# Product with the kernel spectrum formed in place of the mixed stream, in two operations of 1024 elements, with spectra two images ahead in two buffers

## The chip, the core and the metric

The kernel runs on one core of a Trainium2 chip. The metric is the device time of one execution in microseconds. The core has five engines with a queue of instructions each: TensorE (PE, with its weight loads PEld), VectorE (DVE), ScalarE (ACT), GpSimd (POOL) and SyncE (SP), which here only starts transfers. They wait for one another on semaphores.

## The reference

Input x is 8 images of 128 channels, 32 x 32 points. The first layer is an attention block (group norm, Q, K, V, softmax over 1024 points, projection, residual). The second layer is the part that the change touches:

```python
xf = fftshift(fft2(x, norm='ortho'))
kern = _aniso_kernels(params)             # one 7 x 7 kernel per image, from the centre of |xf|
filt = vmap(conv_one)(stacked, kern)      # the spectrum, real and imaginary, convolved with it
rr = einsum('bchw,oc->bohw', real_f, wr)  # channels mixed by wr
ii = einsum('bchw,oc->bohw', imag_f, wr)
return ifft2(ifftshift(complex(rr, ii)), norm='ortho').real + x
```

Convolving a spectrum is a product in the image plane. So the output of an image is x, plus the image mixed by wr times a real function of the 1024 points that belongs to the 7 x 7 kernel (called the kernel's spectrum here and KHAT in the code), less terms for what the convolution with zero padding leaves out at the border.

## The kernel before, in words

The attention part fills the first 335 us or so: a loop over 8 images with 8 tiles of 128 rows each. After it comes the filter part, written out by hand for each engine; the order of its lines is the order of the engine's queue, and nothing else sets it.

X (128 channels by 8 x 1024) holds the output of the attention block, and in the end the result. What the filter part does for image n:

- `mixed_x(n)`: TensorE multiplies X by wr into two PSUM banks, ScalarE copies them to GX (L899). GX has room for all 8 images, and all are there before the stretch in question begins.
- `k_hi(n)` (L880): ScalarE spreads the column n of K3, the kernel's values, over 128 columns of KB. `khat(n, h)`: TensorE multiplies it by a table of cosines into bank 2 + h, for the halves h = 0, 1 of the 1024 points. `khat_copy(n, h)` (L889): ScalarE copies it to KHAT, which lies in the attention part's buffer E, as does KX. Both have room for one image.
- `k_x1(n)` (L1451): GpSimd forms KX = KHAT * GX in two operations of 512 elements (L1458) and adds the first half of X to the first half of KX (L1461). `kx_add(n)` (L1190): VectorE adds the second half (L1193).
- The border terms: `mixed_r(n)` and `r3(n)` (TensorE and ScalarE: the features R mixed by wr to RT, and R3 from them), `v3(n)`, `g_full(n)` (L1175: VectorE writes GF from GC and a mask in MISC, 112 x 448 elements, two buffers), `vt(n)` (TensorE, from GF and V3, into bank 6), `vt_hi(n)` (ScalarE) and `vt_lo(n)` (VectorE, L1173), which split it into two parts.
- `z(n, h)`: nine matmuls per half from the parts of VT into bank h (called Z in the text). `result(n, h)` (L1196): VectorE adds bank h and KX into X (L1203), and SyncE sends it out.

The waits around KX and KHAT: a product of image n waits for the result of image n - 1 in the same half (L1457), a copy of spectrum n for the product of image n - 1 in the same half (L892), the first result for GpSimd's sum, the second for VectorE's (L1199, L1201).

VectorE's queue in the loop, from L1400:

```python
for i in range(B):
    if i + 1 < B:
        vt_lo(i + 1)
    if i + 2 < B:
        g_full(i + 2)
    result(i, 0)
    result(i, 1)
    if i + 1 < B:
        kx_add(i + 1)
```

TensorE's loop is `v3(i + 1)`, `khat(i + 1, 0)`, `khat(i + 1, 1)`, `vt(i + 1)`, then `z(i, 0)`, `z(i, 1)`; the first rounds also hold the last mixes of R and R3.

Of the kernel before, what the change touches and what calls it, by code (L numbers as in the profile page):

```python
# [37 lines left out]
HALF = 512  # L38
# [172 lines left out]
def attention_filter_kernel(nc, x, norm_w, norm_b, wq, bq, wk, bk, wv, bv, wp, bp, w1, b1, w2, b2,  # L211
# [4 lines left out]
    with ExitStack() as ctx:  # L216
# [66 lines left out]
        def bank(i, n=HALF, parts=P):  # L283
            return PS[0:parts, i * HALF:i * HALF + n]
# [22 lines left out]
        def late(name, shape, column):  # L307
# [4 lines left out]
        V3 = late("V3", [P, P], A_HNH + 2 * 4 * CH)  # L312
        GC = late("GC", [P, B * 4 * NZ], A_HNL)
        GX = late("GX", [P, B * N], A_QH)
        KHAT, KX = E[:, 2 * N:3 * N], E[:, 3 * N:4 * N]
        RT = late("RT", [P, B * 4 * P], A_ETL)
        R3 = late("R3", [P, B * P], A_ETL + 6 * N)
        G3 = late("G3", [P, B * P], A_ETL + 7 * N)
# [12 lines left out]
            v_m2 a_mag p_c25 v_c25 p_hid v_hid p_par v_ml v_n2 g_nr a_lam v_ex a_ex p_sum v_k  # L331
            p_k3 a_k3 v_k3 g_g3z p_g v_g a_g3
            p_gx a_gx p_rt a_rt p_r3 a_r3 p_v3 a_v3 v_gf p_vt a_vth v_vtl
            a_kbh p_kh a_kh2 g_kx g_kxx v_kxx p_z v_o""".split()
        s = {n: sem(n) for n in names}

        block = ctx.enter_context(nc.Block())
# [58 lines left out]
        def _(pe):  # L396
# [151 lines left out]
            def mixed_r(n):  # L548

                pe.wait_ge(s["a_ur"], n + 2)  # L550
                if n:
                    pe.wait_ge(s["a_rt"], n)
                else:
                    pe.wait_ge(s["v_lo"], 2 * TILES * B)
                for i, at_ in enumerate((CH, 2 * CH, UO + UA, 0)):
                    c0 = n * UR + at_
                    ins = mm(bank(4)[0:CH, i * P:(i + 1) * P], R[:, c0:c0 + CH], WRT[:], True, True)
                ins.then_inc(s["p_rt"], 1)
# [24 lines left out]
            def vt(n):  # L583

                pe.wait_ge(s["v_gf"], n + 1)
                if n:
                    pe.wait_ge(s["v_vtl"], n)
                for i in range(4):
                    o = bank(6)[0:CH, i * P:(i + 1) * P]
                    g = slice((n % 2 * 4 + i) * CH, (n % 2 * 4 + i + 1) * CH)  # L590
                    ins = mm(o, GF[0:CH, g], RT[0:CH, (4 * n + i) * P:(4 * n + i + 1) * P],
                             True, i < 2)
                    if i == 2:
                        pe.wait_ge(s["a_v3"], n + 1)
                    if i >= 2:
                        w = slice(F_EX + (i - 2) * CH, F_EX + (i - 1) * CH)
                        ins = mm(o, SYF[:, w], V3[:], False, True)
                ins.then_inc(s["p_vt"], 1)

            def khat(n, h):  # L600

                if h == 0:
                    pe.wait_ge(s["a_kbh"], n + 1)
                if n:
                    pe.wait_ge(s["a_kh2"], 2 * n + h - 1)
                else:
                    pe.wait_ge(s["a_gx"], 2 * B - 1 + h)
                    pe.wait_ge(s["d_syn"], 32)
                w = slice(T_COS + h * HALF, T_COS + (h + 1) * HALF)
                mm(bank(2 + h), KB[0:K_ROWS, :], SYH[0:K_ROWS, w], True, True)\  # L610
                    .then_inc(s["p_kh"], 1)
# [179 lines left out]
            v3(0)  # L791
            r3(4)
            vt(0)
            mixed_r(5)

            for i in range(B):
                if i < 2:
                    r3(i + 5)
                if i + 1 < B:
                    v3(i + 1)  # L800
                    khat(i + 1, 0)
                    khat(i + 1, 1)
                    vt(i + 1)
                if i < 2:
                    mixed_r(i + 6)
                z(i, 0)
                z(i, 1)
                if i == 1:
                    r3(7)
# [3 lines left out]
        def _(act):  # L813
# [74 lines left out]

            def khat_copy(n, h):  # L889
                act.wait_ge(s["p_kh"], 2 * n + h + 1)  # L890
                if n:
                    act.wait_ge(s["g_kx"], 2 * n + h - 1)  # L892
                act.activation(KHAT[:, h * HALF:(h + 1) * HALF], bank(2 + h), ACT.Copy)\
                    .then_inc(s["a_kh2"], 1)

            def mixed_x(n):
# [5 lines left out]
            def mixed_r(n):  # L902
                act.wait_ge(s["p_rt"], n + 1)
                act.activation(RT[0:CH, n * 4 * P:(n + 1) * 4 * P], bank(4, HALF, CH), ACT.Copy)\
                    .then_inc(s["a_rt"], 1)
# [20 lines left out]
            def vt_hi(n):  # L926
                act.wait_ge(s["p_vt"], n + 1)
                if n > 1:
                    act.wait_ge(s["p_z"], 2 * n - 2)
                act.activation(VTH[n % 2][0:CH, :], bank(6, HALF, CH), ACT.Copy)\  # L930
                    .then_inc(s["a_vth"], 1)
# [82 lines left out]
            v3_copy(0)  # L1014
            r3_copy(4)
            vt_hi(0)
            mixed_r(5)

            for i in range(B):
                if i < 2:  # L1020
                    r3_copy(i + 5)
                if i + 1 < B:
                    v3_copy(i + 1)
                    khat_copy(i + 1, 0)
                    khat_copy(i + 1, 1)
                    if i + 2 < B:
                        k_hi(i + 2)
                    vt_hi(i + 1)
                if i < 2:
                    mixed_r(i + 6)  # L1030
                if i == 1:
                    r3_copy(7)
# [3 lines left out]
        def _(dve):  # L1036
# [150 lines left out]
                lo(VTL[n % 2][0:CH, :], bank(6, HALF, CH), VTH[n % 2][0:CH, :], "a_vth", n + 1,  # L1187
                   "v_vtl")

            def kx_add(n):  # L1190

                dve.wait_ge(s["g_kx"], 2 * n + 2)
                TT(KX[:, HALF:N], KX[:, HALF:N], X[:, n * N + HALF:(n + 1) * N], ALU.add)\  # L1193
                    .then_inc(s["v_kxx"], 1)

            def result(b, h):  # L1196
                dve.wait_ge(s["p_z"], 2 * b + h + 1)
                if h == 0:
                    dve.wait_ge(s["g_kxx"], b + 1)  # L1199
                else:  # L1200
                    dve.wait_ge(s["v_kxx"], b + 1)  # L1201
                d_ = slice(h * HALF, (h + 1) * HALF)
                TT(X[:, b * N + h * HALF:b * N + (h + 1) * HALF], bank(h), KX[:, d_], ALU.add)\  # L1203
                    .then_inc(s["v_o"], 1)

            def image(b, cur, prev, nxt):
                p = b - 1
# [187 lines left out]
            g_full(0)  # L1395
            g_full(1)
            vt_lo(0)
            kx_add(0)

            for i in range(B):  # L1400
                if i + 1 < B:
                    vt_lo(i + 1)
                if i + 2 < B:
                    g_full(i + 2)
                result(i, 0)
                result(i, 1)
                if i + 1 < B:
                    kx_add(i + 1)


        @block.gpsimd
        def _(pool):
# [37 lines left out]

            def k_x1(n):  # L1451

                for h in range(2):
                    d_ = slice(h * HALF, (h + 1) * HALF)
                    pool.wait_ge(s["a_kh2"], 2 * n + h + 1)
                    if n:
                        pool.wait_ge(s["v_o"], 2 * n + h - 1)  # L1457
                    TT(KX[:, d_], KHAT[:, d_], GX[:, n * N + h * HALF:n * N + (h + 1) * HALF],  # L1458
                       ALU.mult).then_inc(s["g_kx"], 1)
                pool.wait_ge(s["g_kx"], 2 * n + 1)  # L1460
                TT(KX[:, 0:HALF], KX[:, 0:HALF], X[:, n * N:n * N + HALF], ALU.add)\  # L1461
                    .then_inc(s["g_kxx"], 1)

            def image(b, cur, prev, nxt):
                p = b - 1
# [62 lines left out]
```

## Time and profile before

| | us |
|---|---|
| median of 3 runs | 421.76 (421.29 to 422.14) |
| the profiled execution, its own time | 421.87 |
| its span | 420.0 |
| TensorE busy | 395.5 (94%) |
| VectorE busy | 286.0 (68%) |
| ScalarE busy | 241.8 (58%) |
| GpSimd busy | 211.4 (50%) |

The span goes from the first to the last instruction that the profile records; the time of an execution is a little longer. Times in rows count from the start of the span. Busy shares are means over the whole program, whose last 50 us work differently from the rest, so a stretch has to be read by itself. Line numbers are those of the kernel before.

### The profile page before, as it was taken

The numbers are of one execution on the slowest core, as the hardware profiler recorded it, in microseconds if no ns is written. First come the engines' busy times: TensorE is split into PE (matmuls) and PEld (weight loads), VectorE is DVE, ScalarE is ACT, GpSimd is POOL, SyncE is SP. The second block draws the span as 40 slices with busy tenths as digits, with TensorE's granted clock in tenths as the row PEclk, the third lists the DMA queues.
The fourth block names the chain that finished last, engine by engine and source line by source line (L and its number), as shares of the span: only waits on it lengthen the run. The fifth ranks groups of instructions, "written<-read, shape, count | busy, mean of one in ns | idle before, by whom it ended". The sixth has DMA issues, their size and how long they took to land.

```text
span 420.0 us, 6744 instructions
## 1 busy us (share of the span) xinstructions
PE 395.5 (94%) x2237; PEld 326.2 (78%) x2237; DVE 286.0 (68%) x530; ACT 241.8 (58%) x437; POOL 211.4 (50%) x159
## 2 busy tenths in 40 slices
PE   4969999999999999999999999999999999999883
PEld 3547788888888888888888888888888775789772
DVE  2769788949894986788588949885783324137655
ACT  1467667737774666567377837765675265444430
POOL 0066746815861675377257815762662121235664
PEclk9999999999999999999999999999999999999998
DMA  4900340010010001000100100010000270001222
GB/s 114 393 0 2 115 194 0 11 41 0 0 50 0 0 0 50 0 0 0 50 0 0 36 14 0 0 51 0 2 24 2 100 195 2 2 21 80 100 102 100
DMA packets 6495, 19.43 MB, mean 46 GB/s; under 512 B 1680, under 2 KB 2448, under 8 KB 6000
## 3 DMA queue, kind: packets, MB, share of 16 engines
q1 hardware_dynamic: 4384, 12.77, 8.2%
q0 software_dynamic: 800, 5.80, 4.4%
q10 hardware_dynamic: 1296, 0.66, 0.6%
q8 instruction: 9, 0.15, 0.1%
q14 instruction: 6, 0.05, 0.0%
HBM read 15.04 MB, written 4.19 MB: 46 GB/s over the span
## 4 chain that ended last, share of the span: by engine, by line
PE 78%; DVE 8%; ACT 4%; POOL 4%; issue 3%; DMA 1%; DVEq 0%; POOLq 0%; ACTq 0%
PE PS L398 57%; PE PS L471 12%; PE PS L525 7%; POOL E L1458 3%; DVE E L1193 2%; PE PS L516 2%; DVE ETL L1146 1%; DVE NMX L1131 1%; ACT E L862 1%; DVE X L1203 1%; DMA MISC<-in_misc 1%; DVE GF L1180 1%; ACT ETH L871 1%; POOL E L1443 0%; ACT KH L856 0%
## 5 line engine op out<-in xcount | busy, mean ns | idle before, releaser
L1443 POOL TENSOR_TENSOR E<-E,RI 128x1024 f32<-128x1024 f32 x64 | 124.6, 1947 | 110.9 <-DVE RI L1136 110.9
L1131 DVE TENSOR_REDUCE NMX<-PS 128x1 f32<-128x1024 f32 x64 | 77.9, 1217 | 35.1 <-PE PS L398 34.5
L862 ACT ACTIVATE E<-PS,NMX 128x1024 f32<-128x1024 f32 x64 | 71.5, 1116 | 36.4 <-DVE NMX L1131 36.2
L871 ACT ACTIVATE ETH<-PS 128x512 fp32r<-128x512 f32 x128 | 69.5, 597 | 35.0 <-PE PS L471 34.6
L1146 DVE TENSOR_TENSOR ETL<-PS,ETH 128x512 fp32r<-128x512 f32 x128 | 81.9, 681 | 8.5 <-ACT ETH L871 7.6
L471 PE MATMUL PS<-MISC,E 128*128 128x128 f32 x512 | 67.3, 274 | 3.7 <-POOL E L1443 2.7
L471 PEld LDWEIGHTS PS<-MISC,E 128*128 128x128 f32 x512 | 58.7, 140 | 14.9 <-POOL E L1443 5.7
L398 PE MATMUL PS<-ETH,VH 128*128 128x512 f32 x128 | 54.6, 427 | 0.4 <-DVE ETL L1146 0.3
L398 PE MATMUL PS<-ETH,VL 128*128 128x512 f32 x128 | 50.4, 394 | 0.0
L398 PE MATMUL PS<-ETL,VH 128*128 128x512 f32 x128 | 50.0, 391 | 0.0
L398 PE MATMUL PS<-KH,QH 128*128 128x512 f32 x128 | 41.5, 405 | 2.1 <-ACT E L862 1.2
L398 PE MATMUL PS<-KL,QH 128*128 128x512 f32 x128 | 39.9, 393 | 0.0
L398 PE MATMUL PS<-KH,QL 128*128 128x512 f32 x128 | 39.7, 391 | 0.0
L1458 POOL TENSOR_TENSOR E<-E,GX 128x512 f32<-128x512 f32 x16 | 20.2, 1281 | 35.9 <-DVE X L1203 20.9
L398 PEld LDWEIGHTS PS<-KL,QH 128*128 128x128 f32 x128 | 23.9, 188 | 5.8 <-DVE KL L1125 0.6
L398 PEld LDWEIGHTS PS<-ETH,VL 128*128 128x128 f32 x128 | 24.0, 188 | 5.6
L398 PEld LDWEIGHTS PS<-KH,QL 128*128 128x128 f32 x128 | 24.0, 188 | 5.4
L398 PEld LDWEIGHTS PS<-ETH,VH 128*128 128x128 f32 x128 | 24.1, 188 | 5.2 <-DVE ETL L1146 0.8
L398 PEld LDWEIGHTS PS<-KH,QH 128*128 128x128 f32 x128 | 22.6, 189 | 6.7 <-ACT E L862 1.6
L1435 POOL TENSOR_TENSOR VL<-XTF,VH 128x512 fp32r<-128x512 f32 x16 | 20.6, 1288 | 13.2 <-ACT VH L840 13.2
L398 PEld LDWEIGHTS PS<-ETL,VH 128*128 128x128 f32 x128 | 24.2, 189 | 3.3
L398 PE MATMUL PS<-ETH 112*128 112x256 f32 (+2 forms) x64 | 21.6, 358 | 2.0 <-DVE X L1203 2.0
(183 smaller groups left out, 700.0 us busy)
## 6 DMA issues: line engine op xcount, KB each, us to landing
XTF<-in_xt SPq DMA_DIRECT2D x8, 512.0 KB, 3.3
X<-in_x SPq DMA_DIRECT2D x7, 512.0 KB, 6.7
out<-X SPq DMA_DIRECT2D x7, 512.0 KB, 2.6
ANH<-in_anah POOLq DMA_DIRECT2D x1, 1320.0 KB, 6.8
ANL<-in_anal POOLq DMA_DIRECT2D x1, 1320.0 KB, 9.1
ETH<-in_synh POOLq DMA_DIRECT2D x1, 1024.0 KB, 5.1
ETH<-in_gam POOLq DMA_DIRECT2D x1, 900.4 KB, 9.0
ETH<-in_gam POOLq DMA_DIRECT2D x1, 588.0 KB, 6.1
```

The lines of the kernel that those rows point to most:

```text
L398: return pe.matmul(o, a, b_, start=start, stop=stop)
L471: ins = pe.transpose(bank(ET_BANK + k)[:, j * P:(j + 1) * P], E[:, c0:c0 + P], eye)
L516: ins = pe.transpose(bank(MISC_BANK)[:, j * P:(j + 1) * P], T[:, c0:c0 + P], eye)
L525: ins = pe.matmul(o[:, at:at + width], a, r, start=t == FIRST and n == 0, stop=t == LAST and n == 2, skip_group_check=True)
L862: act.activation(E[:, (t % 4) * N:(t % 4 + 1) * N], s_bank(t), ACT.Exp, bias=NMX[:, t % 2:t % 2 + 1], accum_out=RS[:, t % 4:t % 4 + 1]).th ...
L871: act.activation(et[:, h, 4 * k:4 * k + 4, i * P:(i + 1) * P], bank(ET_BANK + k).rearrange("p (j n) -> p j n", j=4), ACT.Copy).then_inc(s[ ...
L1131: dve.tensor_reduce(NMX[:, t % 2:t % 2 + 1], s_bank(t), AX.X, ALU.max, negate=True)\
L1146: TT(etl[part], bank(ET_BANK + k).rearrange("p (j n) -> p j n", j=4), eth[part].bitcast(F32), ALU.subtract).then_inc(s["v_lo"], 1)
L1193: TT(KX[:, HALF:N], KX[:, HALF:N], X[:, n * N + HALF:(n + 1) * N], ALU.add)\
L1435: TT(VL[:, 4 * k:4 * k + 4, :], xt_half(k), VH[:, 4 * k:4 * k + 4, :].bitcast(F32), ALU.subtract).then_inc(s["g_vl"], 1)
L1443: TT(e, e, RI[:, t % 4:t % 4 + 1].broadcast_to([P, N]), ALU.mult)\
L1458: TT(KX[:, d_], KHAT[:, d_], GX[:, n * N + h * HALF:n * N + (h + 1) * HALF], ALU.mult).then_inc(s["g_kx"], 1)
```

## The change

KX is gone. `k_x1(n)` multiplies GX by the spectrum and adds X to it, both in place in GX, each in one operation of 1024 elements; the second waits for the first. VectorE's `kx_add` is gone, and `result` reads GX. KHAT has two buffers, for even and odd images, and a spectrum is formed two images ahead: spectrum 1 before the fifth mix of R, and in round i of the loop spectrum i + 2. A copy of spectrum n waits for the product of image n - 2.

```diff
@@ -312,7 +312,7 @@
         V3 = late("V3", [P, P], A_HNH + 2 * 4 * CH)
         GC = late("GC", [P, B * 4 * NZ], A_HNL)
         GX = late("GX", [P, B * N], A_QH)
-        KHAT, KX = E[:, 2 * N:3 * N], E[:, 3 * N:4 * N]
+        KHAT = (E[:, 2 * N:3 * N], E[:, 3 * N:4 * N])
         RT = late("RT", [P, B * 4 * P], A_ETL)
         R3 = late("R3", [P, B * P], A_ETL + 6 * N)
         G3 = late("G3", [P, B * P], A_ETL + 7 * N)
@@ -331,7 +331,7 @@
             v_m2 a_mag p_c25 v_c25 p_hid v_hid p_par v_ml v_n2 g_nr a_lam v_ex a_ex p_sum v_k
             p_k3 a_k3 v_k3 g_g3z p_g v_g a_g3
             p_gx a_gx p_rt a_rt p_r3 a_r3 p_v3 a_v3 v_gf p_vt a_vth v_vtl
-            a_kbh p_kh a_kh2 g_kx g_kxx v_kxx p_z v_o""".split()
+            a_kbh p_kh a_kh2 g_kx g_kxx p_z v_o""".split()
         s = {n: sem(n) for n in names}
 
         block = ctx.enter_context(nc.Block())
@@ -791,6 +791,8 @@
             v3(0)
             r3(4)
             vt(0)
+            khat(1, 0)
+            khat(1, 1)
             mixed_r(5)
 
             for i in range(B):
@@ -798,8 +800,9 @@
                     r3(i + 5)
                 if i + 1 < B:
                     v3(i + 1)
-                    khat(i + 1, 0)
-                    khat(i + 1, 1)
+                    if i + 2 < B:
+                        khat(i + 2, 0)
+                        khat(i + 2, 1)
                     vt(i + 1)
                 if i < 2:
                     mixed_r(i + 6)
@@ -888,9 +891,9 @@
 
             def khat_copy(n, h):
                 act.wait_ge(s["p_kh"], 2 * n + h + 1)
-                if n:
-                    act.wait_ge(s["g_kx"], 2 * n + h - 1)
-                act.activation(KHAT[:, h * HALF:(h + 1) * HALF], bank(2 + h), ACT.Copy)\
+                if n > 1:
+                    act.wait_ge(s["g_kx"], n - 1)
+                act.activation(KHAT[n % 2][:, h * HALF:(h + 1) * HALF], bank(2 + h), ACT.Copy)\
                     .then_inc(s["a_kh2"], 1)
 
             def mixed_x(n):
@@ -1014,6 +1017,9 @@
             v3_copy(0)
             r3_copy(4)
             vt_hi(0)
+            khat_copy(1, 0)
+            khat_copy(1, 1)
+            k_hi(2)
             mixed_r(5)
 
             for i in range(B):
@@ -1021,10 +1027,11 @@
                     r3_copy(i + 5)
                 if i + 1 < B:
                     v3_copy(i + 1)
-                    khat_copy(i + 1, 0)
-                    khat_copy(i + 1, 1)
                     if i + 2 < B:
-                        k_hi(i + 2)
+                        khat_copy(i + 2, 0)
+                        khat_copy(i + 2, 1)
+                        if i + 3 < B:
+                            k_hi(i + 3)
                     vt_hi(i + 1)
                 if i < 2:
                     mixed_r(i + 6)
@@ -1187,21 +1194,12 @@
                 lo(VTL[n % 2][0:CH, :], bank(6, HALF, CH), VTH[n % 2][0:CH, :], "a_vth", n + 1,
                    "v_vtl")
 
-            def kx_add(n):
-
-                dve.wait_ge(s["g_kx"], 2 * n + 2)
-                TT(KX[:, HALF:N], KX[:, HALF:N], X[:, n * N + HALF:(n + 1) * N], ALU.add)\
-                    .then_inc(s["v_kxx"], 1)
-
             def result(b, h):
                 dve.wait_ge(s["p_z"], 2 * b + h + 1)
                 if h == 0:
                     dve.wait_ge(s["g_kxx"], b + 1)
-                else:
-                    dve.wait_ge(s["v_kxx"], b + 1)
-                d_ = slice(h * HALF, (h + 1) * HALF)
-                TT(X[:, b * N + h * HALF:b * N + (h + 1) * HALF], bank(h), KX[:, d_], ALU.add)\
-                    .then_inc(s["v_o"], 1)
+                d_ = slice(b * N + h * HALF, b * N + (h + 1) * HALF)
+                TT(X[:, d_], bank(h), GX[:, d_], ALU.add).then_inc(s["v_o"], 1)
 
             def image(b, cur, prev, nxt):
                 p = b - 1
@@ -1395,7 +1393,6 @@
             g_full(0)
             g_full(1)
             vt_lo(0)
-            kx_add(0)
 
             for i in range(B):
                 if i + 1 < B:
@@ -1404,8 +1401,6 @@
                     g_full(i + 2)
                 result(i, 0)
                 result(i, 1)
-                if i + 1 < B:
-                    kx_add(i + 1)
 
 
         @block.gpsimd
@@ -1450,16 +1445,12 @@
 
             def k_x1(n):
 
-                for h in range(2):
-                    d_ = slice(h * HALF, (h + 1) * HALF)
-                    pool.wait_ge(s["a_kh2"], 2 * n + h + 1)
-                    if n:
-                        pool.wait_ge(s["v_o"], 2 * n + h - 1)
-                    TT(KX[:, d_], KHAT[:, d_], GX[:, n * N + h * HALF:n * N + (h + 1) * HALF],
-                       ALU.mult).then_inc(s["g_kx"], 1)
-                pool.wait_ge(s["g_kx"], 2 * n + 1)
-                TT(KX[:, 0:HALF], KX[:, 0:HALF], X[:, n * N:n * N + HALF], ALU.add)\
-                    .then_inc(s["g_kxx"], 1)
+                g = GX[:, n * N:(n + 1) * N]
+                pool.wait_ge(s["a_gx"], 2 * n + 2)
+                pool.wait_ge(s["a_kh2"], 2 * n + 2)
+                TT(g, g, KHAT[n % 2], ALU.mult).then_inc(s["g_kx"], 1)
+                pool.wait_ge(s["g_kx"], n + 1)
+                TT(g, g, X[:, n * N:(n + 1) * N], ALU.add).then_inc(s["g_kxx"], 1)
 
             def image(b, cur, prev, nxt):
                 p = b - 1
```

GpSimd, from the last loads of tables to the first image of the products. Before:

```order
L1493 DMA ETH<-in_gam 96x1568
L1494 DMA ETH<-in_gam 96x2401
L1498 TENSOR_TENSOR ML<-ML,PLUS_HALF 49x8
L1458 TENSOR_TENSOR E<-E,GX 128x512 x2
L1461 TENSOR_TENSOR E<-E,X 128x512
```

With the change:

```order
L1484 DMA ETH<-in_gam 96x1568
L1485 DMA ETH<-in_gam 96x2401
L1489 TENSOR_TENSOR ML<-ML,PLUS_HALF 49x8
L1451 TENSOR_TENSOR GX<-GX,E 128x1024
L1453 TENSOR_TENSOR GX<-GX,X 128x1024
```

Three operations of 512 elements per image have become two of 1024, and they write GX; the same follows for each image.

ScalarE, from the copy of mix 4 of R (RT) to the end of round 0 of the loop (V is V3, the first ETH row VT's high part, E the spectrum, the ETH row from K the broadcast for the next one). Before:

```order
L904 ACTIVATE RT<-PS 112x512
L924 ACTIVATE V_51<-PS 128x128
L909 ACTIVATE R_55<-PS 128x128
L930 ACTIVATE ETH<-PS 112x512
L904 ACTIVATE RT<-PS 112x512
L909 ACTIVATE R_55<-PS 128x128
L924 ACTIVATE V_51<-PS 128x128
L893 ACTIVATE E<-PS 128x512 x2
L886 ACTIVATE ETH<-K 96x128
L930 ACTIVATE ETH<-PS 112x512
```

With the change:

```order
L907 ACTIVATE RT<-PS 112x512
L927 ACTIVATE V_51<-PS 128x128
L912 ACTIVATE R_55<-PS 128x128
L933 ACTIVATE ETH<-PS 112x512
L896 ACTIVATE E<-PS 128x512 x2
L889 ACTIVATE ETH<-K 96x128
L907 ACTIVATE RT<-PS 112x512
L912 ACTIVATE R_55<-PS 128x128
L927 ACTIVATE V_51<-PS 128x128
L896 ACTIVATE E<-PS 128x512 x2
L889 ACTIVATE ETH<-K 96x128
L933 ACTIVATE ETH<-PS 112x512
```

Two copies and a broadcast stand ahead of the copy of mix 5 that stood behind it; round 0 keeps its three, which now belong to spectrum 2.

VectorE, from the first GF to the results of image 0 and 1 (ETL is VT's low part). Before:

```order
L1180 TENSOR_TENSOR GF<-GC,MISC 112x448 x2
L1173 TENSOR_TENSOR ETL<-PS,ETH 112x512
L1193 TENSOR_TENSOR E<-E,X 128x512
L1173 TENSOR_TENSOR ETL<-PS,ETH 112x512
L1180 TENSOR_TENSOR GF<-GC,MISC 112x448
L1203 TENSOR_TENSOR X<-PS,E 128x512 x2
L1193 TENSOR_TENSOR E<-E,X 128x512
```

With the change:

```order
L1187 TENSOR_TENSOR GF<-GC,MISC 112x448 x2
L1180 TENSOR_TENSOR ETL<-PS,ETH 112x512 x2
L1187 TENSOR_TENSOR GF<-GC,MISC 112x448
L1202 TENSOR_TENSOR X<-PS,GX 128x512 x2
L1180 TENSOR_TENSOR ETL<-PS,ETH 112x512
```

The additions into E are gone; the rest keeps its order, and the results read GX.

## Rows read from the trace of the kernel before

**Rows 1.** The page's head and its first line of busy time (us, share, instructions)

```profile
span 420.0 us, 6744 instructions
...
PE 395.5 (94%) x2237; PEld 326.2 (78%) x2237; DVE 286.0 (68%) x530; ACT 241.8 (58%) x437; POOL 211.4 (50%) x159
```

**Rows 2.** Stretch table, 400 to 410: length, busy us by engine, clock, DMA share, GB/s

```profile
400.00:410.00 10.00, 8.86 (x62) 7.70 (x60) 5.78 (x7) 3.81 (x8) 7.46 (x6) 1.00 0.26 105
```

**Rows 3.** Chain of waits, one image (start us, us, engine, tile, line)

```profile
399.36 0.61 DVE X L1203
...
400.11 0.50 POOL E L1458
...
401.34 1.31 POOL E L1458
...
402.68 1.40 DVE E L1193
...
404.36 0.14 DVE ETL L1173
...
404.96 0.61 DVE GF L1180
405.57 0.61 DVE X L1203
```

**Rows 4.** Instructions by line: ns minimum/median/maximum, first and last start, form

```profile
L1458 POOL TENSOR_TENSOR E<-E,GX x16: 1257/1280/1298, 364.6 to 413.2; 128x512 f32<-128x512 f32 x16
...
L1461 POOL TENSOR_TENSOR E<-E,X x8: 1258/1284/1301, 367.1 to 414.5; 128x512 f32<-128x512 f32 x8
...
L1443 POOL TENSOR_TENSOR E<-E,RI x64: 1883/1893/2385, 24.5 to 315.6; 128x1024 f32<-128x1024 f32 x64
...
L1414 POOL MEMSET MINUS_HALF<- x1: 98/98/98, 0.8 to 0.8; 128x1 f32 x1
...
L1193 DVE TENSOR_TENSOR E<-E,X x8: 681/1760/1768, 369.0 to 414.6; 128x512 f32<-128x512 f32 x8
...
L1203 DVE TENSOR_TENSOR X<-PS,E x16: 673/676/691, 374.4 to 416.8; 128x512 f32<-128x512 f32 x16
```

**Rows 5.** Timeline of GpSimd and VectorE; page's group of the attention's low parts

```profile
402.59 1.30 POOL L1461 TENSOR_TENSOR E<-E,X 128x512 f32<-128x512 f32 x1
...
402.68 1.76 DVE L1193 TENSOR_TENSOR E<-E,X 128x512 f32<-128x512 f32 x1 [2.11 <-POOL E L1458]
...
L1146 DVE TENSOR_TENSOR ETL<-PS,ETH 128x512 fp32r<-128x512 f32 x128 | 81.9, 681 | 8.5 <-ACT ETH L871 7.6
```

**Rows 6.** Timeline of TensorE's weight loads, 375 to 382 (start us, us, count)

```profile
375.44 0.53 PEld L398 LDWEIGHTS PS<-RT,SYF 112*128 112x128 f32 x4
375.89 0.30 PEld L398 LDWEIGHTS PS<-R,G 128*128 128x128 f32 x2
...
376.46 0.84 PEld L398 LDWEIGHTS PS<-RT,GF 112*112 112x112 f32 x6
...
377.90 0.94 PEld L398 LDWEIGHTS PS<-WRT,R 128*112 128x112 f32 x8
378.77 0.19 PEld L398 LDWEIGHTS PS<-ETH 112*128 112x128 f32 x1
...
381.57 0.53 PEld L398 LDWEIGHTS PS<-RT,SYF 112*128 112x128 f32 x4
```

**Rows 7.** Timeline, the start of the stretch: spectrum 0, mix 5, first Z

```profile
363.90 1.10 ACT L893 ACTIVATE E<-PS 128x512 f32<-128x512 f32 x2
...
368.66 0.60 ACT L904 ACTIVATE RT<-PS 112x512 f32<-112x512 f32 x1 [0.28 <-PE PS L398]
...
372.64 0.19 PEld L398 LDWEIGHTS PS<-ETH 112*128 112x128 f32 x1
```

**Rows 8.** Timeline, the end: the last results and their transfers

```profile
416.22 1.27 DVE L1203 TENSOR_TENSOR X<-PS,E 128x512 f32<-128x512 f32 x2
...
416.93 0.95 SPq L390 DMA_DIRECT2D out<-X  x2
```

## The prediction

> **What bounds the kernel now.** I read the page first: 420.0 us of span, TensorE busy for 94% of it [rows 1]. That share is an average. The change touches the last 50 us alone, so I went to the stretches there, and TensorE is no longer full: 8.86 of 10 us from 400 to 410, at a granted clock of 1.00, while GpSimd is busy for 7.46 [rows 2]. The chain of waits then shows which work ends last. From one image to the next it goes (399.36 to 405.57, 6.21 us) [rows 3]: the first result (0.61) frees the first half of KX; GpSimd starts its products 0.13 later (400.11), two of them up to 402.65; VectorE adds x to the second half (402.68, counted for 1.68 until the next step at 404.36); then, in VectorE's own queue, the low part of VT (0.60), GF (0.61), and the result of the next image. TensorE is a passenger: it waits for GF and for the results. So the ring result, KX, products, add, VT low part, GF, result sets 6.21 us per image, and it exists because there is one KX buffer.
>
> The add in that ring is dear for another reason. Alone it took 681 ns; its median is 1760 [rows 4]. One case is laid out: GpSimd's own add runs from 402.59 for 1.30, VectorE's starts at 402.68 and ends at 404.44, 0.55 after GpSimd's end [rows 5]. It reads two operands in SBUF. VectorE operations that read one operand in PSUM show nothing of the kind: the results are at 673 to 691 [rows 4], the 128 low parts of the attention part at 681 on average, with GpSimd busy beside many of them [rows 5].
>
> **The change part by part.** Removed: the KX buffer with its two waits (products for results, spectrum copies for products inside one image), eight adds on VectorE (8 x 1.76 at most), and eight 512-element GpSimd adds with sixteen 512-element products. Added: sixteen 1024-element GpSimd operations, and one spectrum (two matmuls, two copies, one broadcast of K) moved ahead of R's fifth mix.
>
> *The ring* goes. A result now waits for its own matmuls and for a sum that depends on nothing but spectrum copies made two images ahead. What is late next is one of two engines.
>
> *TensorE, per image:* V3 and the two spectrum matmuls 375.89 to 376.46, 0.57; VT 376.46 to 377.90, 1.44; the output product Z 378.77 to 381.57, 2.80 [rows 6]. Together 4.81. R3 (375.44 to 375.89) is 0.45 and a mix of R (377.90 to 378.77) 0.87.
>
> *GpSimd, per image:* two operations of 1024 elements with two full inputs, which the trace doesn't have. Above: twice a 512-element operation, 2 x 1.28 = 2.56. Below: the attention's 1024-element product, whose second operand is one broadcast column, 1.89 [rows 4]. I take a value near the upper end, since the inputs are full there and the form is the same: two products back to back took 2.53 (400.11 to 402.65 [rows 3]), less one start, which the smallest operation of GpSimd (98 ns) [rows 4] bounds: 2.43. The sum now waits for the product just before it (before, it waited for the one before that, long done), so I add 0.11, a little under the 0.13 of the hand-over between engines above. A pass is 2 x 2.43 + 0.11 = 4.97.
> The Trainium skill (GPSIMD Engine Reference, 3.1) gives 4497 ns for such an addition of 2048 elements; with this trace's 1.28 for 512 an estimate on a straight line is 2.35, which would end this sum 1.2 us earlier.
>
> *GF, the operation that takes the add's place at the port.* It too has two SBUF operands (GC and MISC), 0.61 us. Before, it always ran while GpSimd stood still for KX (at 404.96 [rows 3], with GpSimd done at 402.59 + 1.30 = 403.89 [rows 5]). Now GpSimd is nearly always busy, so each of GF 2 to 7 has to be let in between two of its operations, by the way the add was. It then holds GpSimd for 0.61 - 0.13 = 0.48 (0.13 being the 0.68 of the add alone less the 0.55 it still took after GpSimd's end), in place of the 0.11: a pass with GF in it is 5.34, longer than TensorE's 4.81. So GpSimd sets the pace.
> The Trainium skill has this as a rule that speaks against the change (SBUF — State Buffer, "Who interferes with whom"): a VectorE instruction with two SBUF inputs and a GpSimd one that reads SBUF exclude each other for the whole instruction. The add at 402.68 agrees; that GF does so too no row shows.
>
> *The start.* Both halves of spectrum 0 are copied from 363.90 for 1.10 [rows 7], so the first pass starts at 365.13. ScalarE now does two copies and a broadcast (some 1.2) between VT's first copy and the copy of mix 5 (368.66) [rows 7]; the spectra's two matmuls lie in TensorE's own wait before it. R3 of image 5 and the first Z (372.64) come some 0.9 later, 373.5. This costs nothing if GpSimd binds; it is in the sum below if TensorE does.
>
> *The sum.* Passes 0 and 1 are over before GF 2 is asked for: 365.13 + 2 x 4.97 = 375.07. Passes 2 to 6 with GF: + 26.70 = 401.77. Product 7: 404.20. GF 7: 404.68. VT 7 1.44, Z of image 6 and of image 7 5.60, the last result 0.69, hand-overs some 0.2: 412.6. Before, the last result ended at 416.22 + 1.27 = 417.49, and 2.51 later, with the last transfer out, the span [rows 8]. That tail stays. Gain 4.9: the span goes from 420.0 to 415.1, and the profiled execution's 421.87 to **417.0**. It lies 0.11 over the median of the runs (421.76), which changes nothing.
> By the bound of 2.56 per operation the same sum gives 414.6 for the last result, 419.0 in all.
>
> **The rivals.**
> *TensorE binds* (GpSimd's operation at 2.2 or less, or GF isn't held up). Then from 373.5: eight Z 22.4; before them in turn 3.33 (R3, V3 and spectra, VT, mix), 2.01 + 0.45, three times 2.01, and 1.67; 0.9 for the end: 410.3. Gain 7.2, **414.7**. For: the 1.89 of the broadcast product, and no row with GF beside GpSimd. Against: all two-input operations of 512 elements are at 1.28 [rows 4].
> *GF is let in late.* Between a sum and the next product GpSimd waits for nothing, so GF gets in only once per pass. Where it has just missed the gap it waits up to 5 us, and TensorE behind it. Some of GF 2 to 7 hit this while the two engines find their step: one or two us more than the forecast, 418 to 420.
> *Slower: GF is not let in at all while GpSimd has work.* The 0.11 between product and sum may be no gap for VectorE: no row shows VectorE waiting with GpSimd's next operation already queued (in the add's case GpSimd had run out). Place: VectorE's queue, with VT's low parts and results behind GF. GpSimd works until spectra run out. GF 2 then follows sum 2, 365.13 + 3 x 4.97 = 380.0. From there two images take: GF 0.61, VT 1.44, Z 2.80, spectra matmuls 0.57, copies 1.2, a pass 4.97 and hand-overs, 11.8, so 5.9 each. GF 7 starts at 409.5, and 8.4 later, as above, the last result: 417.9, 0.4 later than before, **422.3**; with 2.56 per operation 423.5. It decides from the point where GF has to wait for the second operation of the pass each time.
> *It doesn't do what it says:* the spectra aren't ahead. A copy waits for the product two images back, which by the sum is over more than 3 us before it; I give this no share of its own.
>
> **How the numbers follow.** GpSimd's pace with GF let in: 0.50, 417.0 (own range 415.3 to 419.0, from 2.35 and 2.56). TensorE: 0.26, 414.7. GF late: 0.11, 419. GF shut out: 0.10, 422.3. The remaining 0.03 is no change: two losses that cancel. Within 0.2% (0.8 us, about what a measurement of this kernel can tell from no change) is that 0.03; faster is 0.50 + 0.26 + 0.11 = 0.87; slower 0.10. The range takes in the first three: 414.0 to 420.0.
>
> **What would show it.** The spacing of results in the steady part: 5.3 if GpSimd binds, 4.8 if TensorE does, 5.9 if GF is shut out. GpSimd's 1024-element operations at 2.43. GF longer than 0.61, ending 0.5 after an operation of GpSimd, mostly between product and sum. TensorE waiting for GF some 0.5 per image. The first product at 365.1, the first Z at 373.5. I am wrong if GF stays at 0.61 with GpSimd busy beside it, if an operation takes other than 2.35 to 2.56, or if results get longer than 0.69, which would mean that a PSUM operand doesn't keep them off the port.

## The result and the profile after

The changed kernel takes 415.32 us (median of 4 executions, 415.24 to 415.43) against 421.79 for the kernel before: ratio 0.9844, 95% interval 0.983 to 0.9858, so 6.5 us less. The forecast was 417.0, with a range of 414.0 to 420.0. Everything below compares positions inside one profiled execution each (span 413.6 us after, 420.0 before).

The head of the page after, and the stretches that answer to [rows 1] and [rows 2] (length, busy us of PE, PEld, DVE, ACT and POOL, granted clock, share of the transfer engines, GB/s):

```profile
span 413.6 us, 6712 instructions
...
PE 395.3 (96%) x2237; PEld 327.5 (79%) x2237; DVE 281.2 (68%) x522; ACT 241.3 (58%) x437; POOL 220.8 (53%) x151
```

```profile
380.00:390.00 10.00, 10.00 (x73) 9.31 (x72) 7.29 (x8) 4.39 (x11) 9.84 (x4) 1.00 0.13 52
390.00:400.00 10.00, 10.00 (x71) 9.07 (x70) 7.30 (x8) 4.28 (x10) 9.84 (x5) 1.00 0.27 107
400.00:410.00 10.00, 9.52 (x65) 8.63 (x64) 6.76 (x8) 1.22 (x3) 5.32 (x3) 1.00 0.33 132
```

TensorE is full until 400, and GpSimd is as good as full too (9.84 of 10): two engines at nearly the same pace. Between 400 and 410 TensorE has 9.52 where it had 8.86 [rows 2], and the last result ends at 411.14.

The chain of waits after, from the last piece before the first Z to the end (start us, us, engine, tile, line); it answers to [rows 3]:

```profile
370.19 29.53 PE PS L398 x214
399.72 0.02 issue
399.75 0.61 ACT ETH L933
...
400.98 2.19 DVE GF L1187
403.18 0.04 issue
403.22 7.20 PE PS L398 x48
410.42 0.02 issue
410.45 0.69 DVE X L1202
```

The turning ring of [rows 3] is gone. TensorE alone carries the chain for 29.5 us, through the rounds of images 0 to 4 and into 5. Then GF 7, the last one (images count from 0), takes 2.19 us and TensorE stands for it, and after it TensorE runs to the last result, which ends at 411.14 where it ended at 417.49 [rows 8]. The chain follows semaphores only, so it doesn't show what GF 7 itself stood for; the timelines below do.

The results of images 1 to 5 (start us, us) come 5.08 to 5.09 apart, where the kernel before had 6.21:

```profile
382.75 1.28 DVE L1202 TENSOR_TENSOR X<-PS,GX 128x512 f32<-128x512 f32 x2
387.83 1.28 DVE L1202 TENSOR_TENSOR X<-PS,GX 128x512 f32<-128x512 f32 x2
392.92 1.28 DVE L1202 TENSOR_TENSOR X<-PS,GX 128x512 f32<-128x512 f32 x2
398.01 1.28 DVE L1202 TENSOR_TENSOR X<-PS,GX 128x512 f32<-128x512 f32 x2
403.09 1.28 DVE L1202 TENSOR_TENSOR X<-PS,GX 128x512 f32<-128x512 f32 x2
```

That is GpSimd's pace and not TensorE's, because each pair of results stands behind a GF in VectorE's queue.

By line (ns minimum/median/maximum), the new GpSimd operations, GF, and the results; they answer to [rows 4]:

```profile
L1451 POOL TENSOR_TENSOR GX<-GX,E x8: 2346/2401/2779, 365.3 to 400.3; 128x1024 f32<-128x1024 f32 x8
...
L1453 POOL TENSOR_TENSOR GX<-GX,X x8: 2358/2634/2652, 367.7 to 402.8; 128x1024 f32<-128x1024 f32 x8
...
L1187 DVE TENSOR_TENSOR GF<-GC,MISC x8: 618/1582/2510, 359.3 to 401.0; 112x448 f32<-112x448 f32 x8
...
L1202 DVE TENSOR_TENSOR X<-PS,GX x16: 675/678/692, 375.2 to 410.4; 128x512 f32<-128x512 f32 x16
```

GF went from 0.61 to a median of 1.58 and a maximum of 2.51. The results, with one operand in PSUM, stay at 0.68 although GpSimd is busy beside them. The last two passes of GpSimd, and below them the GFs in them (start us, us):

```profile
395.19 2.41 POOL L1451 TENSOR_TENSOR GX<-GX,E 128x1024 f32<-128x1024 f32 x1
397.68 2.65 POOL L1453 TENSOR_TENSOR GX<-GX,X 128x1024 f32<-128x1024 f32 x1
400.29 2.40 POOL L1451 TENSOR_TENSOR GX<-GX,E 128x1024 f32<-128x1024 f32 x1
402.76 2.63 POOL L1453 TENSOR_TENSOR GX<-GX,X 128x1024 f32<-128x1024 f32 x1
```

```profile
396.11 1.97 DVE L1187 TENSOR_TENSOR GF<-GC,MISC 112x448 f32<-112x448 f32 x1
...
400.98 2.18 DVE L1187 TENSOR_TENSOR GF<-GC,MISC 112x448 f32<-112x448 f32 x1
```

GF of 396.11 is asked for while the product runs (to 397.60) and ends at 398.08, 0.48 after it; the sum that follows the product takes 2.65 where it takes 2.38 alone. The next GF waits a little longer (2.18), because GpSimd turns every 5.1 us and TensorE every 4.8: the two slide against each other until TensorE is held up. GpSimd itself works without a break from its first product (365.25) to the end of product 7 (402.69), where GF 7 gets in.

### The profile page after: what moved, and what is told of

Its sections match the earlier page's. It is cut to its first block, busy times and chain, and to the rows that moved or that the text cites. A ratio compares the mean times of both kernels' runs of the same rounds, so it can differ in the third digit from the quotient of the medians.

```text
span 413.6 us, 6712 instructions
## 1 busy us (share of the span) xinstructions
PE 395.3 (96%) x2237; PEld 327.5 (79%) x2237; DVE 281.2 (68%) x522; ACT 241.3 (58%) x437; POOL 220.8 (53%) x151
## 4 chain that ended last, share of the span: by engine, by line
PE 88%; ACT 5%; DVE 4%; DMA 1%; issue 1%; POOL 1%; ACTq 0%
PE PS L398 66%; PE PS L471 13%; PE PS L525 7%; PE PS L516 2%; DVE ETL L1153 1%; DMA MISC<-in_misc 1%; ACT E L865 1%; ACT ETH L874 1%; DVE NMX L1138 1%; DVE GF L1187 1%; ACT E L896 0%; POOL E L1438 0%; ACT KH L859 0%; ACT QH L859 0%; ACT L941 0%
## 5 line engine op out<-in xcount | busy, mean ns | idle before, releaser
L1451 POOL TENSOR_TENSOR GX<-GX,E 128x1024 f32<-128x1024 f32 x8 | 19.5, 2438 | 15.4 <-ACT E L896 15.4
L1143 DVE RECIPROCAL RI<-RS 128x1 f32<-128x1 f32 x64 | 10.4, 162 | 17.0 <-ACT E L865 15.4
```

Source lines behind the costliest of these rows:

```text
L1143: dve.reciprocal(RI[:, t % 4:t % 4 + 1], RS[:, t % 4:t % 4 + 1])\
L1451: TT(g, g, KHAT[n % 2], ALU.mult).then_inc(s["g_kx"], 1)
```

## The experiments

Each of them is compared with the kernel before on the same chip; the chip differs between groups of experiments, and the median of the kernel before with it (421.7 to 422.1). So the ratios are the fair comparison between rows, and most of their intervals near 0.982 and 0.984 touch. Since the stretch begins up to 1.2 us earlier or later from one profiled execution to another (the first copy of spectrum 0 at 363.26 to 364.42), I also use a length inside each profile: from the start of the first Z to the start of the last result. It is 44.2 before (372.64 to 416.8) and 36.93 after (373.52 to 410.45). The table gives the median time, the ratio with its 95% interval, and that length; each experiment follows below.

| kernel | us | ratio | first Z to last result |
|---|---|---|---|
| the change | 415.32 | 0.9844 (0.983 to 0.9858) | 36.93 |
| in place only | 414.32 | 0.9824 (0.9811 to 0.9837) | 36.60 |
| in place, GFs ahead | 414.17 | 0.9818 (0.9799 to 0.9837) | 36.58 |
| one spectrum buffer | 415.12 | 0.9842 (0.9829 to 0.9856) | 37.3 |
| GFs ahead | 414.44 | 0.9821 (0.9808 to 0.9835) | 36.12 |
| no sum | 414.48 | 0.9819 (0.9804 to 0.9834) | 36.13 |
| other order | 415.96 | 0.9854 (0.9839 to 0.9869) | 37.80 |
| GFs ahead, other order | 414.39 | 0.9821 (0.9808 to 0.9834) | 36.12 |
| before, GFs ahead | 419.55 | 0.9949 (0.9936 to 0.9963) | 42.0 |
| four halves | 433.29 | 1.0262 (1.0248 to 1.0276) | 55.19 |
| four halves, GFs ahead | 414.68 | 0.9839 (0.9822 to 0.9855) | 36.11 |
| halves in turn | 414.70 | 0.9838 (0.982 to 0.9855) | 36.13 |
| sum one later | 415.4 to 424.1 | see below | 44.66 in one of the long executions |

### Which part of the change carries the gain

**In place only.** The kernel before, with products and sums written into GX. The results read GX (not shown), and since nothing frees it any more, the first product waits once for all copies to GX (not shown), which are long done; nothing else is changed.

```diff
-                    if n:
-                        pool.wait_ge(s["v_o"], 2 * n + h - 1)
-                    TT(KX[:, d_], KHAT[:, d_], GX[:, n * N + h * HALF:n * N + (h + 1) * HALF],
-                       ALU.mult).then_inc(s["g_kx"], 1)
+                    g = GX[:, n * N + h * HALF:n * N + (h + 1) * HALF]
+                    TT(g, KHAT[:, d_], g, ALU.mult).then_inc(s["g_kx"], 1)
...
-                TT(KX[:, HALF:N], KX[:, HALF:N], X[:, n * N + HALF:(n + 1) * N], ALU.add)\
+                g = GX[:, n * N + HALF:(n + 1) * N]
+                TT(g, g, X[:, n * N + HALF:(n + 1) * N], ALU.add)\
```

> The kernel before with one thing changed: product and sum are written in place in GX, so the products no longer wait for results. 512-element operations, VectorE's add, one spectrum buffer and one image ahead stay. Theory (the KX ring was the whole cost): TensorE binds at 4.81 per image from a first Z at 372.6, last result near 409.5, time 413.9 to 414.6, so as good as the change or better. Rival (the two buffers or the larger operations carry the gain): 418 or more.

Measured 414.32, a ratio of 0.9824. The theory holds: this one step gives the whole gain, and about 1 us more by the median and by the profile (from the first copy of spectrum 0 to the end of the last result 46.03, with the change 47.13), though the two ratio intervals overlap a little. Its chain of waits is TensorE without a break, from before 385 to the last result:

```profile
384.89 24.22 PE PS L398 x169
409.11 0.02 issue
409.13 0.69 DVE X L1204
```

VectorE's add, 1.76 in the kernel before, now takes 0.68, since it comes when GpSimd has run out of work. So the two spectrum buffers, the move to two images ahead and the larger operations were not needed for this gain.

**One spectrum buffer.** The change without its second buffer and without the move ahead.

```diff
-                if n > 1:
-                    act.wait_ge(s["g_kx"], n - 1)
-                act.activation(KHAT[n % 2][:, h * HALF:(h + 1) * HALF], bank(2 + h), ACT.Copy)\
+                if n > 0:
+                    act.wait_ge(s["g_kx"], n)
+                act.activation(KHAT[0][:, h * HALF:(h + 1) * HALF], bank(2 + h), ACT.Copy)\
...
-                    if i + 2 < B:
-                        khat(i + 2, 0)
-                        khat(i + 2, 1)
+                    khat(i + 1, 0)
+                    khat(i + 1, 1)
```

> The changed kernel with one spectrum buffer and spectra one image ahead; products in place in 1024-element operations stay. Theory: the copies of the next spectrum lie beside GpSimd's sum, TensorE's round of 4.81 has room for the rest, and the first Z is back at 372.6: 414.4 to 415.3. Rival (two buffers are needed): copies 1.2 and a pass 4.8 in a row, 6.0 or more per image, 420 or more.

415.12, in the expected range, and the change's own time within what can be told apart. Its chain ends in GpSimd's products and sums, 5.08 us a turn, and the last results wait 2.0 us for the last sum. The second buffer saves that wait, and the first Z, 0.8 later with it (9.51 after the first copy of spectrum 0, here 8.74), gives that back in part; in time the two kernels can't be told apart.

**Before, GFs ahead.** The kernel before with the edit of the next section.

> The kernel before with all GFs written before the loop; the KX ring stays. Theory (the ring of the chain of waits is right): each turn but the last loses GF's 0.61, 5.6 per image, 6 x 0.6 = 3.6 us less, 418.2. Rival (the ring is set by something else): no change, 421.8.

419.55, 2.3 us less, where I expected 3.6. The ring turns in 5.66 us (the chain of waits, from one result to the next), where it turned in 6.21:

```profile
397.38 0.68 DVE X L1207
...
398.20 0.51 POOL E L1460
...
399.43 1.30 POOL E L1460
...
400.76 1.40 DVE E L1197
...
402.44 0.14 DVE ETL L1179
...
403.04 0.69 DVE X L1207
```

So the ring was read rightly, but I had counted 0.6 for six turns. The last turn had no GF in it already, three lost 0.54 to 0.55, and the first two only 0.18 and 0.36, by the starts of the products (374.90, 381.05, 386.87 here).

### What bounds the changed kernel

**GFs ahead.** All eight GFs are written before the loop, into eight buffers.

```diff
+        GFB = [GF[:, 0:4 * CH], GF[:, 4 * CH:8 * CH], GF_A[:], GF_B[:]] \
+            + [T[:, k * 4 * CH:(k + 1) * 4 * CH] for k in range(2)] \
+            + [GF_C[:, k * 4 * CH:(k + 1) * 4 * CH] for k in range(2)]
...
-            g_full(0)
-            g_full(1)
+            for n in range(B):
+                g_full(n)
...
-                if i + 2 < B:
-                    g_full(i + 2)
```

> The changed kernel with all eight GFs written before the loop, into eight buffers, so that none meets a running GpSimd operation. Theory (TensorE binds up to image 5, and the wait of GF for the port delays TensorE only at the end): GF is 0.61 each time, GpSimd's pass 4.75, TensorE waits for nothing after the first Z at 373.5, the last result comes about 1.0 us earlier, time 414.3. Rival (GpSimd's own pace binds, GF does not matter): 415.3, no change against the changed kernel.

414.44, as expected; from the first Z to the last result 36.12, 0.81 less than the change. The chain has no GF in it and no GpSimd:

```profile
369.45 39.42 PE PS L404 x282
408.86 0.02 issue
408.89 0.69 DVE X L1206
```

GpSimd's turn without GF is 4.81 (products at 393.80 and 398.61), so GF cost it 0.28 a turn.

**No sum.** GpSimd's additions of x are left out, and the results wait for the product in their place.

```diff
-                pool.wait_ge(s["g_kx"], n + 1)
-                TT(g, g, X[:, n * N:(n + 1) * N], ALU.add).then_inc(s["g_kxx"], 1)
```

> The changed kernel without the addition of x in GpSimd (the output lacks the residual x of the filter layer): GpSimd has eight operations in place of sixteen. Theory: it is then idle half of the time, GF waits at most for the rest of one product, TensorE binds throughout: last result 1.0 earlier, 414.3. Rival (GpSimd's pace of 5.1 per image set the time of the changed kernel throughout): two us or more earlier, 413 or less.

414.48, as expected, and 36.13 from the first Z on: the same floor, reached by halving GpSimd's work in place of moving GF. GF still waits here (1.29 to 1.33), but never long enough to hold TensorE. Together the two show that 36.1 us is TensorE's own length, and that the changed kernel lies 0.8 above it.

**Other order**, alone and with the GFs ahead: ScalarE copies spectrum 1 after mix 5.

```diff
-            khat_copy(1, 0)
-            khat_copy(1, 1)
-            k_hi(2)
             mixed_r(5)
+            khat_copy(1, 0)
+            khat_copy(1, 1)
+            k_hi(2)
```

> The changed kernel with ScalarE's copies of spectrum 1 put behind the copy of mix 5. Theory: the first Z begins near 372.7 in place of 373.5, but GpSimd starts as before and GF 7 is let in when its product 7 ends (402.7), so the end stays: 415.3, at most 0.3 less. Rival (TensorE's start is what counts): 414.5.

> Both edits: all GFs before the loop and the copies of spectrum 1 behind mix 5. Theory: TensorE binds all the way from a first Z at 372.7, so both terms count: 1.0 and 0.8 less than the changed kernel, 413.5. Rival (GpSimd binds once TensorE starts earlier): its eight passes end at 365.25 + 38.0 = 403.3, results by 411.1 as now, 414.3 to 415.3.

415.96 and 414.39: both expectations missed. (414.39 lies in the range of the rival named there, but not for its reason: the chain is TensorE's in one piece of 38.74 us.) The first Z does not come earlier. TensorE's spectrum 2 waits for the broadcast of K, which now stands behind the copies (0.4 us there), and from the first copy of spectrum 0 to the first Z it takes 9.69 us where the change takes 9.51. Meanwhile GpSimd waits 0.92 for spectrum 1, and its product 1 starts at 370.81 in place of 370.00:

```profile
370.81 2.36 POOL L1451 TENSOR_TENSOR GX<-GX,E 128x1024 f32<-128x1024 f32 x1 [0.92 <-ACT E L896]
```

That lost time passes to the end where GF ties GpSimd to TensorE (37.80, 0.87 more than the change), and not where it doesn't (36.12). So in the changed kernel GpSimd's delay is the kernel's. I had looked at one wait in TensorE's queue and not at the one behind it.

### When VectorE is let in

**Four halves.** The change with GpSimd's two operations split into four of 512. Only the lines added are shown; the copies of the spectrum and the results count halves in their waits accordingly.

```diff
+                for h in range(2):
+                    d_ = slice(h * HALF, (h + 1) * HALF)
+                    pool.wait_ge(s["a_kh2"], 2 * n + h + 1)
+                    TT(g[:, d_], g[:, d_], KHAT[n % 2][:, d_], ALU.mult).then_inc(s["g_kx"], 1)
+                for h in range(2):
+                    d_ = slice(h * HALF, (h + 1) * HALF)
+                    pool.wait_ge(s["g_kx"], 2 * n + h + 1)
+                    TT(g[:, d_], g[:, d_], x_[:, d_], ALU.add).then_inc(s["g_kxx"], 1)
```

> The changed kernel with GpSimd's two 1024-element operations split into four of 512. Theory (GpSimd's pace sets the last images): a pass is 4 x 1.25 plus GF's 0.4, 5.3 to 5.4 in place of 5.1, so the end comes 1 to 2 us later, 416.3 to 417.3. Rival (shorter operations let GF in sooner, and that is worth more): 415.3 or less.

433.29, 11.4 us slower than the kernel before, and neither theory saw it. GF twice stands for 9 to 11 us. VectorE's timeline:

```profile
373.91 10.77 DVE L1187 TENSOR_TENSOR GF<-GC,MISC 112x448 f32<-112x448 f32 x1
...
395.36 0.96 DVE L1187 TENSOR_TENSOR GF<-GC,MISC 112x448 f32<-112x448 f32 x1
...
400.19 8.83 DVE L1187 TENSOR_TENSOR GF<-GC,MISC 112x448 f32<-112x448 f32 x1
```

GpSimd's, of the same kernel:

```profile
379.29 2.47 POOL L1453 TENSOR_TENSOR GX<-GX,E 128x512 f32<-128x512 f32 x2
381.73 2.47 POOL L1457 TENSOR_TENSOR GX<-GX,X 128x512 f32<-128x512 f32 x2
393.32 2.53 POOL L1453 TENSOR_TENSOR GX<-GX,E 128x512 f32<-128x512 f32 x2 [9.12 <-ACT E L896]
395.80 2.90 POOL L1457 TENSOR_TENSOR GX<-GX,X 128x512 f32<-128x512 f32 x2
```

The GF of 373.91 ends at 384.68, 0.48 after GpSimd has done its last available operation (384.20) and ran out of spectra. In between, GpSimd passed from one operation to the next eight times, and VectorE was not let in. Meanwhile TensorE stands still behind GF, and GpSimd then waits 9.12 for a spectrum. The waits of TensorE in this profile (us in total, times, longest):

```profile
PE PS L398 <- DVE GF L1187: 13.9, 2, 7.3
```

After each of the two stops TensorE also works at a lower granted clock for a while: 0.68 on the mean from 385 to 390, and 0.50, the lower of its two levels, from 410 to 415. Before each it had stood for most of the 5 us. The standing and the lower clock together are the loss. This is the forecast's slower rival, GF shut out while GpSimd has work, in a kernel that differs from the change only in how GpSimd's work is cut.

**Four halves, GFs ahead.**

> Four GpSimd operations of 512 elements per image as in the kernel that took 433.3, but with all GFs written before the loop. Theory (its whole loss is GF standing before a port that GpSimd never leaves): a pass is 5.0, TensorE binds, 414.4 as with two operations of 1024. Rival (four operations cost by themselves): 417 or more.

414.68, first Z to last result 36.11: four operations cost nothing by themselves. All of the some 18.5 us between the two kernels came of GF's waits, 13.9 of it as TensorE's standing. The rest would be its lower clock after them; this is by elimination and not shown by a run.

**Halves in turn.** Four operations of 512, as product, sum, product, sum (again only the lines added).

```diff
+                for h in range(2):
+                    d_ = slice(h * HALF, (h + 1) * HALF)
+                    pool.wait_ge(s["a_kh2"], 2 * n + h + 1)
+                    TT(g[:, d_], g[:, d_], KHAT[n % 2][:, d_], ALU.mult).then_inc(s["g_kx"], 1)
+                    pool.wait_ge(s["g_kx"], 2 * n + h + 1)
+                    TT(g[:, d_], g[:, d_], x_[:, d_], ALU.add).then_inc(s["g_kxx"], 1)
```

> Four operations of 512 per image, but in the order product, sum, product, sum, so that each sum waits for the product just before it; GF stays in the loop. Theory (the idle moment of 0.1 before such a sum is what lets VectorE in): GF waits at most some 2.5, no GF over 3.2, GpSimd's pass 5.1 to 5.5, time 414.8 to 416. Rival (with operations of 512 VectorE is shut out whatever the order): 425 or more.

414.70, a little under the expected 414.8 to 416 and at TensorE's floor (36.13). The same operations in another order, and no GF is longer than this:

```profile
L1187 DVE TENSOR_TENSOR GF<-GC,MISC x8: 618/1086/1757, 359.4 to 401.0; 112x448 f32<-112x448 f32 x8
```

What differs is the order and, with it, that each sum waits for the product just before it; no run changes the one without the other. The timeline shows a step of 1.34 from product to sum where it is 1.22 to 1.25 elsewhere: GpSimd is idle for some 0.08.

**Sum one later.** The change's operations of 1024, with the product of image n + 1 ahead of the sum of image n.

```diff
+            k_x1(0)
+            for n in range(B):
+                if n + 1 < B:
+                    k_x1(n + 1)
+                x_sum(n)
```

> Operations of 1024 elements as in the change, but the product of image n + 1 stands ahead of the sum of image n, so no operation waits for the one just before it; GF stays in the loop. Theory (the idle moment is what lets VectorE in): GF waits until GpSimd has run out of spectra, 9 us or more once or twice, time 425 or more. Rival (the size of the operations is what counts): GF waits at most 2.4, time 415 to 416.5.

Its ten executions fall into two groups: three at 415.4 to 416.2 and seven at 422.5 to 424.1. The profiled one is of the second group (422.88), and shows why. VectorE's GF 3 and GF 7, and GpSimd beside GF 7:

```profile
380.08 4.24 DVE L1187 TENSOR_TENSOR GF<-GC,MISC 112x448 f32<-112x448 f32 x1
...
402.42 6.17 DVE L1187 TENSOR_TENSOR GF<-GC,MISC 112x448 f32<-112x448 f32 x1
```

```profile
398.38 2.76 POOL L1456 TENSOR_TENSOR GX<-GX,X 128x1024 f32<-128x1024 f32 x1
401.10 2.40 POOL L1451 TENSOR_TENSOR GX<-GX,E 128x1024 f32<-128x1024 f32 x1
403.46 4.64 POOL L1456 TENSOR_TENSOR GX<-GX,X 128x1024 f32<-128x1024 f32 x2
```

GF 7 waits through the rest of a product and two whole sums, until GpSimd is done (408.10 + 0.49). TensorE stands for GF for 5.7 us in all and is at a granted clock of 0.62 from 405 to 410. None of the three short executions was profiled; that GF was let in sooner in them is inferred. So being shut out does not depend on 512 elements; what the two bad kernels share is that no operation of GpSimd waits for the one just before it, over a long unbroken run of them. It came less often and cost less than I expected (425 or more), and whether it comes differs between executions of one kernel. The expectation was right in kind and too high.

What decides more finely stays open. In the two profiles (four halves, and this one) GF was also let in without such a wait, each time at the first or second change of operation after GpSimd had been idle (395.80 and 420.14 in the four halves; 374.01, 392.84 and 398.38 here), and shut out at the third or a later one. The in-place kernel agrees: none of its operations waits for the one just before it either, but GpSimd idles every image, and all six of its GFs in the loop (0.88 to 0.92) got in at the second change after that. No run shows why.

**In place, GFs ahead.**

> The kernel before with products and sums in place in GX and all GFs before the loop: one spectrum buffer, 512-element operations, VectorE's add. Theory: the in-place kernel without that edit (414.3) already had TensorE unbroken from the first Z to the last, so this adds nothing: 414.1 to 414.5. Rival (GF's waits still cost there): 0.5 or more less.

414.17, first Z to last result 36.58 against 36.60: as the theory had it, in the in-place kernel GF costs nothing, because GpSimd, with one spectrum buffer, idles every image. Its length is 0.5 above the 36.1 of the kernels that form spectrum 2 before the first Z (the two matmuls of spectrum 7 stand in its last round, which is 0.46 longer, and are missing there in the others), and, like the kernel before, it has its first Z some 0.8 sooner after spectrum 0. It is level with the best of the others (414.4), all of them some 1 us ahead of the change and 7.5 ahead of the kernel before.

## Why the prediction was right, and what it had wrong

*The ring.* Right, as the step that carries the gain: with in-place products alone the chain is TensorE's, and the kernel before turns in 5.66 without GF.

*TensorE's round of 4.81.* Right. Its own end was put at 410.3. In the changed kernel, the first Z at 373.52 plus TensorE's 36.12 plus the last result's 0.69 is 410.33; the measured end is 411.14.

*Which engine binds.* Right in mechanism, with two terms too large, and this is most of the 1.7 us between 417.0 and 415.3. The sum said that GpSimd works without a break and that GF 7 gets in when its product 7 ends, and so it was: GpSimd is unbroken from 365.25 to 402.69, the results come 5.08 to 5.09 apart (the forecast's sign for GpSimd was 5.3, for TensorE 4.8), and a GpSimd that starts product 1 late by 0.92 ends the kernel 0.87 later (other order). From GF 7's entry to the end it is 8.44 us, 8.4 in the forecast. What was too large: the operation was put at 2.43 with 0.11 for the wait, a pass of 4.97; measured 2.35 to 2.42 and 0.08, a pass of 4.75 at first and 4.81 later. That is 1.25 us over the whole sum. GF was put at 0.48 in place of 0.11, so 0.37 more; measured 0.28 more between product and sum, and 0.41 the one time (374.19) it got in between a sum and the next product. That is 0.38. With these 1.63 less and a start 0.12 later, GF 7 was let in at 402.7 in place of 404.2.

*How TensorE meets it.* Wrong in the forecast's list of signs: TensorE was to wait for GF some 0.5 per image. It is full until 400, since its 4.8 is so close to the pass of 5.1 that the two slide through the loop, and TensorE's matmuls stand for GF once, for 0.5 us at the very end. So GpSimd's pace costs the kernel only 0.8 us over TensorE's own length.

*GF waits for GpSimd as the add did.* Right, and it was the step that no row of the kernel before showed: GF ended 0.48 after GpSimd's operation, and its median went from 0.61 to 1.58. The rule named there (the Trainium skill, SBUF — State Buffer, "Who interferes with whom") agrees with the trace after; it does not speak of an engine that is kept out from one operation to the next.

*The start.* The first Z came at 373.52, as forecast (373.5). From the first copy of spectrum 0 to it it is 9.51 where it was 8.74, so the copies cost 0.77, near the forecast's 0.9, and the stretch began 0.11 later in this execution.

*Costs at nothing.* The results stayed at 0.68, and the tail at 2.46 (2.51 before). Right.

*The rivals.* TensorE binding (414.7) is what the kernel does with the GFs ahead (414.44); the change lies 0.8 above it. GF let in late (419) did not happen: GF 2 got in between a sum and a product, and no GF took over 2.51. GF shut out (422.3) did not happen either. The kernels whose sum waits for the product just before it never showed it; whether the idle moment is the reason, and not the order, is not shown. The mechanism is real all the same: it took some 18.5 us in the kernel of four halves, and 7 to 9 in most executions of the one with late sums. That GF would be let in was taken over from the add, for which GpSimd had run out of work; no row showed it for a GpSimd whose next operation is already queued, so in this the forecast was in part lucky.

## What to carry to other kernels

A single buffer that is filled by one engine and freed by another's last step makes a ring; look for another place to write the result (here the operand itself) before adding buffers or moving work ahead, and try that one step alone, since here it gave all of the gain and the rest gave about 1 us back. Before one filler engine is made nearly fully busy, list the short operations of VectorE with two SBUF operands: here GF then waited for GpSimd each time, and doing all GFs earlier, while GpSimd was idle, took that away. Cutting the filler's work into smaller pieces did not by itself make it give way; with each sum waiting for the product just before it, it did.

## What the hardware showed that I had not expected

A VectorE operation with two SBUF operands was kept from starting across eight successive GpSimd operations, for 10.77 us in place of 0.61, and got in only when GpSimd had nothing left. In kernels where each sum of GpSimd waits for the product just before it, with 0.08 us idle between them, the longest such operation, its wait included, was 2.51 (beside operations of 1024 elements) or 1.76 (of 512). With late sums, one and the same kernel takes 415.4 in some executions and 424.1 in others. GpSimd's operation of 1024 elements with two full inputs takes 2.35 to 2.42, less than two of 512 (2 x 1.28) but hardly less than two back to back (2.49 to 2.54).
